# Where the softmax division is done in a four-layer kernel: small products into a bank, or a repeated reciprocal that is transposed

## The reference

```python
scores = q @ k.T + mask            # 512 x 512 for each head and batch
p      = exp(scores - max(scores)) # per row
out    = (p @ v) / sum(p)          # the kernel divides after the product with v
```

## Time and profile before

| | us |
|---|---|
| median of 3 runs | 2855.88 |
| lowest, highest | 2855.48, 2857.81 |
| the profiled execution, its own time | 2853.02 |
| its span, first to last instruction | 2851.0 |
| PE, DVE, ACT, POOL busy | 2561.1, 1257.6, 1133.4, 263.4 |
| mean granted share of PE's clock | 0.943 |

### The profile page before, as it was taken

The page is one execution under the profiler, slowest core; times in us unless marked ns, Lnnn a source line. Parts: engine busy times, 40 slices in busy tenths (PEclk is TensorE's granted clock), DMA queues, the critical chain, the costliest instruction groups (busy, mean ns, idle before and its releaser), DMA issues.

```text
span 2851.0 us, 32766 instructions
## 1 busy us (share of the span) xinstructions
PE 2561.1 (90%) x13072; PEld 1549.5 (54%) x13072; DVE 1257.6 (44%) x2490; ACT 1133.4 (40%) x2422; POOL 263.4 (9%) x233
## 2 busy tenths in 40 slices
PE   5678989999999949999999789999999849999998
PEld 1244444545545518888888444444444418888733
DVE  1146455444344453434433144636356464444334
ACT  0256466544343331111111255747556352222263
POOL 2223123012011000000000110101000000000021
PEclk8879999999999979999999889999989979999999
DMA  8000000000000010000100200000000101000001
GB/s 298 27 1 1 1 1 23 1 8 8 1 8 1 1 44 23 23 23 23 37 9 0 80 0 1 1 1 1 1 1 1 42 19 44 15 30 1 0 15 44
DMA packets 35687, 61.24 MB, mean 21 GB/s; under 512 B 5184, under 2 KB 18032, under 8 KB 35024
## 3 DMA queue, kind: packets, MB, share of 16 engines
q1 hardware_dynamic: 31984, 47.20, 5.0%
q0 software_dynamic: 3552, 11.96, 1.1%
HBM read 52.86 MB, written 4.19 MB: 20 GB/s over the span
## 4 chain that ended last, share of the span: by engine, by line
PE 53%; DVE 5%; ACT 5%; issue 0%; POOL 0%; DVEq 0%; ACTq 0%; POOLq 0%
PE banks L970 18%; PE banks L983 12%; PE banks L441 10%; PE banks L682 3%; PE banks L675 2%; PE banks L695 2%; PE banks L527 1%; DVE sb_Pr L740 1%; DVE sb_PT L747 1%; PE banks L81 1%; PE banks L598 1%; ACT sb_Pr L765 1%; PE banks L591 1%; PE banks L87 1%; ACT sb_experts L609 1%; DVE sb_Pb L99 0%
## 5 line engine op out<-in xcount | busy, mean ns | idle before, releaser
L970 PE MATMUL banks<-sb_H,sb_Ws 128*128 128x512 f32 x2304 | 536.9, 391 | 31.1 <-DVE sb_Ws L1021 30.9
L970 PEld LDWEIGHTS banks<-sb_H,sb_Ws 128*128 128x128 f32 x2304 | 435.2, 189 | 123.8 <-issue 32.5
L765 ACT ACTIVATE sb_Pr<-sb_Pr,sb_nmax 128x512 f32<-128x512 f32 (+3 forms) x512 | 326.0, 638 | 117.4 <-DVE sb_nmax L740 115.2
L682 PEld LDWEIGHTS banks<-sb_ident,sb_Pr 128*128 128x128 f32 x2176 | 251.6, 147 | 210.4 <-issue 90.0
L682 PE MATMUL banks<-sb_ident,sb_Pr 128*128 128x128 f32 x2176 | 327.5, 292 | 28.2 <-ACT sb_PT L770 21.9
L675 PE MATMUL banks<-sb_R 32*128 32x512 f32 (+4 forms) x1280 | 305.9, 602 | 45.1 <-DVE sb_nmax L740 30.3
L747 DVE COPY sb_PT<-banks 128x512 f32<-128x512 f32 (+3 forms) x320 | 195.3, 610 | 333.4 <-PE banks L682 330.8
L740 DVE CUSTOM_DVE_ANT_0 sb_Pr<-banks,sb_bias 128x512 f32<-128x512 f32 (+3 forms) x512 | 290.9, 581 | 92.9 <-PE banks L675 91.9
L983 PE MATMUL banks<-sb_hidH,sb_Ws 128*128 128x512 f32 x1024 | 325.2, 389 | 0.0
L770 ACT ACTIVATE sb_PT<-banks 128x512 f32<-128x512 f32 (+3 forms) x320 | 169.2, 529 | 349.5 <-PE banks L682 348.8
L441 PE MATMUL banks<-sb_hN,sb_W 128*128 128x512 f32 x576 | 273.3, 622 | 12.3 <-ACT sb_hN L382 9.6
(11 more groups left out here) (172 smaller groups left out, 2575.4 us busy)
## 6 DMA issues: line engine op xcount, KB each, us to landing
sb_WM<-in_L_cond_Wfc SPq DMA_DIRECT2D x16, 512.0 KB, 4.2
sb_WM<-in_L_cond_Wada SPq DMA_DIRECT2D x6, 1024.0 KB, 5.1
sb_x<-in_x SPq DMA_DIRECT2D x4, 1024.0 KB, 13.6
sb_WM<-in_L_cond_Wg SPq DMA_DIRECT2D x8, 512.0 KB, 3.4
sb_WM<-in_L_cond_Wu SPq DMA_DIRECT2D x8, 512.0 KB, 4.4
sb_WM<-in_L_cond_Wd SPq DMA_DIRECT2D x8, 512.0 KB, 3.6
out_x<-sb_x SPq DMA_DIRECT2D x4, 1024.0 KB, 4.5
sb_W<-in_L_cond_Wqkv POOLq DMA_DIRECT2D x1, 3072.0 KB, 10.5
```

What stands on the lines that cost most here:

```text
L682: mm = e.transpose(bank[:, j * P:(j + 1) * P], k.Pr[:, n % 6, j * P:(j + 1) * P], k.ident[:])
L765: ins = e.activation(prob, prob if s.biased else k.bank(n % 4)[:, 0:s.width(u)], ACT.Exp, bias=s.stat(k, k.nmax, b, u), scale=-1.0 if s.bi ...
L970: mm = e.matmul(k.bank(s.ups * t + w), lhsT, rhs, start=i == 0, stop=i == len(mats) - 1)
```

## The change

The division is done in another order, and by other instructions:

- `out` no longer copies the values. A new step `expand` (POOL) repeats each reciprocal over its head's channels and writes the result, 128 x 512, into the channel block of `A`.
- `spread` (PE) transposes that tile by four blocks of 128x128 into bank 4 or 5, in all three attentions.
- `out` (ACT) now copies this bank into `A`. It stands right behind the spread, a round later than before.
- `divide` (DVE) multiplies `A` by bank 6, the values' own bank. So the reader of the values is now `divide`, and that of the spread's bank is `out`.
- `recip` and `expand` are listed behind the values of the round.

All calls of `after(...)` are also written in another way: it returns a list of the waits, and the caller issues them. The waits that result are the same; this makes up most lines of the diff and is left out here.

```diff
         else:
-            after(s.name, b, "recip", u)
-            bank = s.tab.claim(s, b, kind, u, after)
+            for due in after(s.name, b, "expand", u):
+                e.wait_ge(*due)
+            bank = s.tab.claim(e, s, b, kind, u, after)
             for i in range(TT):
-                for hl in range(s.per):
-                    o = s.column(u, i, hl)
-                    mm = e.matmul(bank[hl * s.dv:(hl + 1) * s.dv, i * P:(i + 1) * P],
-                                  k.rsum[:, b % 2, o:o + 1].to_broadcast([P, s.dv]), k.ident[:], start=True, stop=True)
+                mm = e.transpose(bank[:, i * P:(i + 1) * P], s.out(b, u)[:, i * P:(i + 1) * P], k.ident[:])
         mm.then_inc(k.done["pe"], 1)
 
     def reader(s, kind, u):
-        return {"turn": ("copy", u), "spread": ("divide", u), "values": ("out", u // 2)}[kind]
...
+        return {"turn": ("copy", u), "spread": ("out", u), "values": ("divide", u // 2)}[kind]
...
         else:
-            after(s.name, b, "out", u)
-            after(s.name, b, "spread", u)
-            ins = e.tensor_tensor(s.out(b, u), s.out(b, u), s.tab.at[(s.name, b, "spread", u)], ALU.mult)
+            for due in after(s.name, b, "out", u):
+                e.wait_ge(*due)
+            for due in after(s.name, b, "values", 2 * u + 1):
+                e.wait_ge(*due)
+            ins = e.tensor_tensor(s.out(b, u), s.out(b, u), s.tab.at[(s.name, b, "values", 2 * u)], ALU.mult)
         ins.then_inc(k.done["dve"], 1)
+
+    def pool(s, k, e, b, kind, c, after):
+
+        for due in after(s.name, b, "recip", c):
+            e.wait_ge(*due)
+        for key in s.out_free(b):
+            for due in after(*key):
+                e.wait_ge(*due)
+        o = slice(s.column(c, 0, 0), s.column(c + 1, 0, 0))
+        e.tensor_copy(s.out(b, c).rearrange("p (n d) -> p n d", d=s.dv),
+                      k.rsum[:, b % 2, o].unsqueeze(2).to_broadcast([P, D // s.dv * TT // C, s.dv]))\
+            .then_inc(k.done["pool"], 1)
...
         else:
-            after(s.name, b, "values", 2 * u + 1)
-            for key in s.out_free(b):
-                after(*key)
-            ins = e.activation(s.out(b, u), s.tab.at[(s.name, b, "values", 2 * u)], ACT.Copy)
+            for due in after(s.name, b, "spread", u):
+                e.wait_ge(*due)
+            ins = e.activation(s.out(b, u), s.tab.at[(s.name, b, "spread", u)], ACT.Copy)
...
         for h, b, c in spreads:
-            seq.extend([(h, b, "pe", "spread", c), (h, b, "dve", "divide", c)])
+            seq.extend([(h, b, "pe", "spread", c), (h, b, "act", "out", c), (h, b, "dve", "divide", c)])
         spreads = []
         for h, b, u in units(t - 1)[3:]:
             if (u + 1) % h.G == 0:
                 g = h.group(u)
                 seq.append((h, b, "pe", "values", g))
                 if g % 2:
-                    seq.extend([(h, b, "act", "out", g // 2), (h, b, "dve", "recip", g // 2)])
                     spreads.append((h, b, g // 2))
+        for h, b, u in units(t - 1)[3:]:
+            if (u + 1) % (2 * h.G) == 0:
+                seq.extend([(h, b, "dve", "recip", h.group(u) // 2), (h, b, "pool", "expand", h.group(u) // 2)])
```

232 lines of the change are left out of this document (146 added, 86 removed).

## The result

The changed kernel takes 2901.59 us (median of 4 executions, 2900.71 to 2902.07), the kernel before, on the same chip, 2855.68 us. The ratio is 1.0161, with a 95% interval of 1.0146 to 1.0176: slower by 45.9 us. The forecast was 2896 us, in a range of 2872 to 2918. The profiled execution took 2900.71 us, of which 2898.9 are span; that is 47.7 us more than the profiled execution of before.

What follows compares the result with a forecast made beforehand. The prediction took TensorE, busy 90% of the span, to bound the kernel. heads1 +32.5, heads2 +7.6 and heads0 0 made +40 us on 2853.0, thus 2893, plus 2.9 for the median: 2896 us, range 2872 to 2918.

Steps and rivals of the forecast that it cites:

- its sign of being right: heads1 30 to 36 us longer, with 16 PE waits released by the division, some 35 us in all.
- Bank 6 in heads1: Next values wait for the division: seven late exps 2.48 us each, two behind squares 4.56, seven with free ACT about 1.31.
- The walk: Place-by-place count of new delays in the three attention stages: +40 us in sum, 2896 us; chance 0.70.
- Places behind the squares: Two heads1 places where four norm squares stand between exp and copy in ACT's order: +4.56 us each, 9.1 us.
- Taken back, -3 us: heads1: PE's later waits shorten and recover 3 us of the 35.5, leaving +32.5.
- The clock, 0: Fewer products and more transposes on PE leave its granted clock unchanged, judged by 2175 to 2250 at 1.00.
- this rival: Clock falls by 0.03 in the three stages: 38 us more, 2934 us; chance 0.04.
- PE's saving: Transposes in place of small products relieve PE of 0.40 us per division, 48 times, 19 us at most.
- heads2, +7.6: heads2: later divisions delay DVE's max and the fourth turn's bank; +7.6 us, ends 0 and 15.
- heads0, 0: heads0: six covered places save 0.4 us each, nine DVE delays cost 2.4 us; sum 0, ends -5 and +8.
- POOL: 48 new copies at 1.3 us or less, PE never idle for them; 0, with +3 us kept for the range.
- Only the saving counts (2837): Rival: values behind the spread are covered, so only PE's -19 us remains, 2837 us; chance 0.05.

Runs made afterwards that it cites:

- the run with short stalls: Kernel before, small products kept, but in heads1 the values behind a spread wait for its division: 2872.29 us.
- the run with the old order: Kernel before with only the small products replaced by POOL's repeat and PE transposes, its order and division kept: 2826.23 us.
- The run without transposes: Kernel before, small products kept, with ACT's copy of the values in heads2 listed beside the spread, so its division is late: 2861.91 us.
- long stalls and no transposes: Kernel before, small products kept, with heads1's values waiting for the division and ACT's copy listed beside the spread: 2896.41 us.
- the two early orders: Changed kernel with repeat a round earlier, transposes and ACT's copy before the block's last values; division behind those values or the round's last max: 2838.82 and 2836.91 us.

## Why the prediction was right, and where it was not

The total came out, 45.9 us measured for 40 forecast, and the mechanism in heads1 is shown by taking it away. But the total is better than its parts, and in that it was lucky: a loss to the clock of 18.4 us was put at nothing, while heads2's delays were put 6 us too high and the part behind the last division came out 3.5 us shorter. heads1 alone came out at +42 to +43 us, outside the 30 to 36 that the prediction names as its sign of being right.

- **Bank 6 in heads1.** Right as to mechanism, place and size. Sixteen waits for the division, up to 4.5 us; without them the stage is 40.5 us shorter. The walk's 35.5 us are the later starts of the values behind the spread. By the weight loads, from the spread to the values, these are 34.5 us. (The PE row's 36.1 counts from the end of the transposes and is another measure.) A place with a late exp cost 2.27 us for 2.48, since ACT's copy starts 0.1 us before the exp's read ends and the handovers are a little shorter; one with a free ACT 1.25 to 1.66 for 1.31.
- **Places behind the squares.** The walk's +4.56 was right for the stall (4.34 by the loads) and too small for its effect. The values behind it took 3.48 us for 1.9, and the next divisions were 5.9 and 7.0 us later.
- **Taken back, -3 us.** Hardly. The waits on ACT's exp (L725) fell from 12.6 to 10.4 us in the stage, but 0.9 of that (2.83 to 1.94 us, at 614) lies ahead of the first wait for bank 6. That leaves 1.3 us, and the run with short stalls shows nothing taken back (16.9 us for 17.1).
- **The clock, 0.** This is the step that failed. "I expect no change" rested on a stretch at 1.00, of which it says that most of its 538 matmuls are transposes. They are 176 (L682), a third, so the row shows less than was read from it. It also answers only the question whether transposes lower the clock; they don't, as the run with the old order shows. The question to ask was what the new stalls do to it: 10.8 us more are lost in heads1 and 7.6 in heads2. The prediction's own sign for this rival, PE rows that get longer at the same order, has come up (442 ns for 382), but the rival had the wrong cause and twice the size.
- **PE's saving.** 0.40 us per division, 19 us at most. The total of the queue's relief is near that, some 20 us with the old order, but it is shared out otherwise: more in heads0 and heads2, since the loads alone (0.81) were taken for the time in which the small products hold the queue (1.01), though the row stood there, and less in heads1, where the values' loads follow the transposes' first by 0.59 us and not 0.42.
- **heads2, +7.6.** Measured +10.1, but not by the walk. The run without transposes shows that a late division costs 7.7 us before any saving, where the walk had 7.6 + 6.4 = 14; the clock filled the gap.
- **heads0, 0.** -0.2 to -2 us by the two counts. With the old order it would have gained 8.4, so here too the new order spends what the new instructions save.
- **The rest.** "The MLPs as before" holds for those in the middle, but the part behind the last division is 3.5 us shorter (592.5 for 596.0), since that division itself is late. The sum had no term for it.
- **POOL.** At most 1.3 us, measured 0.614; PE waited for it 0.6 us in all (the L757 row). Right, but for "never idle for POOL", and a copy of 1037 ns changed nothing either.
- **Only the saving counts (2837).** As a rival it was given little for this order, rightly; it is what the same instructions do in the old order, and they do better, 2826.

The Trainium skill ("TensorE: Matmul & The Clock Gate", Part 1, on the gate's oscillation in real kernels) describes a PE that waits between bursts, drops to the lower clock and starts each burst at it. It bore on this change more than the page's remark on transposes. The traces agree with it for the waits of over 4 us, each with a stretch at the lower level beside it, and in part for those of 2.15 to 2.4 us (values of 442 ns for 382 in the changed kernel, 423 with long stalls and no transposes). They don't for those of 1.1 us (393 ns).

## What to carry to other kernels

A cheaper way to compute a factor is worth its saving only in an order that adds no wait: ask which buffer the new last reader frees, and what stands next in the queue of the engine that bounds. When a change puts stalls of two microseconds and more in front of a busy TensorE, expect some of the work behind them to run at half clock, and look for that in the same instructions' mean duration. Here that was some 10 us on top of 34.5. A stage's mean clock alone can hide it, as in heads2. If an order costs in one stage and gains in another, give each stage its own.

## What the hardware showed that was not expected

- A wait of 4.51 us was followed by 3.6 us at a granted clock of 0.53. Fifteen stalls of 1.1 us left the stage's clock at 0.97; fifteen of which nine were longer, two of 4.2 and seven of 2.15 us on PE's row, took it to 0.95, with no transpose involved.
- In heads2 the granted clock was 0.96 or 0.97 with transposes alone or lateness alone, 0.94 with both, and 0.93 or 0.94 in the two early orders; no run explains it.
- The clock also differs between executions of one kernel: the transposes in the old order took 2825 to 2826 us at 0.946 or 0.947 in three executions and 2833 to 2834 at 0.943 in two.
- POOL's repeat of a column over 32 or 64 places, 128x512, takes 614 ns, and a sum of the column with itself 1037, where its product of two full tiles takes 1276.
